# Local attention block: a second buffer for the cosine products of k and for its weights, and the probabilities multiplied on GpSimd

## The reference, cut to what matters

```python
def attn_layer(x, Wqkv, qs, ksc, Wo):
    q, k, v = jnp.split(x @ Wqkv, 3, -1)          # then 16 heads of 64
    q = l2norm(q) * qs
    k = l2norm(k) * ksc
    q = q * cos * scale + rotate_half(q) * sin * scale
    k = k * cos * inv + rotate_half(k) * sin * inv
    out = local_attention(q, k, v)                # softmax over 64 keys per query
    return out @ Wo

for i in range(DEPTH):                            # 6
    x = attn_layer(shift_tokens(x), Wqkv[i], ...) + x
    x = ffn_layer(shift_tokens(x), ...) + x
```

## Time and profile before

| | |
|---|---|
| median of 3 runs | 4544.87 us (4536.48 to 4553.36) |
| the profiled execution, its time | 4562.02 us |
| the profiled execution, its span | 4560.2 us |
| mean granted TensorE clock | 0.959 of full speed |
| first local block, `by_cosine` of k first and last | 591 us to 2214 us |
| second local block, the same | 2849 us to 4471 us |

### The profile page before, as it was taken

One profiled execution on the slowest core, in us unless ns is written; L12 is line 12 of the kernel. 1 busy time (PEld: TensorE's weight loads), 2 busy tenths in 40 slices (PEclk: granted clock), 3 DMA queues, 4 the chain that ended last, 5 costly groups with the idle time before them and its releaser, 6 DMA issues. The chain is left out here.

```text
span 4560.2 us, 151802 instructions
## 1 busy us (share of the span) xinstructions
PE 4106.5 (90%) x66856; PEld 2986.7 (65%) x66856; DVE 3629.6 (80%) x4427; ACT 2586.8 (57%) x3022; POOL 2608.7 (57%) x3233
## 2 busy tenths in 40 slices
PE   8999968999999999999878887798999999999997
PEld 5665557777777777777633333677777777777775
DVE  5536568888888898898668884888888888888885
ACT  3414335666666656656427773465656656566664
POOL 2103167677767766767424441776767767677673
PEclk8989989999999999999969997999999999999999
DMA  4304232323223232232100001223232232323221
GB/s 143 118 10 151 86 94 65 90 70 90 65 70 93 67 87 68 74 87 69 38 10 1 1 1 39 72 58 98 66 89 72 69 86 67 92 68 91 66 67 37
DMA packets 164545, 316.97 MB, mean 70 GB/s; under 512 B 38760, under 2 KB 42480, under 8 KB 156848
## 3 DMA queue, kind: packets, MB, share of 16 engines
q1 hardware_dynamic: 153520, 241.18, 19.8%
q0 software_dynamic: 10368, 66.06, 4.5%
HBM read 92.03 MB, written 20.05 MB: 25 GB/s over the span
## 5 line engine op out<-in xcount | busy, mean ns | idle before, releaser
L695 PE MATMUL psum<-loc_w_hl,loc_z_lo 128*128 128x512 f32 x1152 | 513.9, 446 | 33.5 <-DMA loc_w_hl<-parted 25.3
L1077 POOL TENSOR_TENSOR loc_rc_k<-loc_rc_k,loc_rs_k 128x1024 f32<-128x1024 f32 x192 | 456.5, 2378 | 85.2 <-DVE loc_rs_k L1187 84.8
L697 PE MATMUL psum<-loc_w_hl,loc_z_hi 128*128 128x512 f32 x1152 | 460.5, 400 | 5.9 <-issue 5.7
L1077 POOL TENSOR_TENSOR loc_rc_q<-loc_rc_q,loc_rs_q 128x1024 f32<-128x1024 f32 x192 | 464.4, 2419 | 0.0
L1173 DVE TENSOR_REDUCE loc_ssq<-loc_sq 128x16 f32<-128x1024 f32 x384 | 463.6, 1207 | 0.0
L696 PE MATMUL psum<-loc_w_hl,loc_z_hi 128*128 128x512 f32 x1152 | 460.4, 400 | 1.3 <-issue 1.3
L941 ACT ACTIVATE loc_sq<-psum 128x1024 f32<-128x1024 f32 x192 | 196.6, 1024 | 466.9 <-PE psum L697 461.9
L1168 DVE TENSOR_TENSOR loc_rc_k<-psum,loc_rot 128x1024 f32<-128x1024 f32 x192 | 234.6, 1222 | 257.2 <-POOL loc_qk_k L1083 227.9
L792 PE MATMUL psum<-loc_PT,loc_V 64*64 64x32 f32 x24576 | 407.1, 220 | 15.3 <-issue 15.0
L792 PEld LDWEIGHTS psum<-loc_PT,loc_V 64*64 64x64 f32 x24576 | 383.3, 135 | 41.6 <-issue 18.2
L812 PEld LDWEIGHTS psum<-loc_outT,loc_wo 128*128 128x128 f32 x3072 | 382.3, 196 | 25.5 <-issue 8.6
(11 more groups left out here) (198 smaller groups left out, 9914.2 us busy)
## 6 DMA issues: line engine op xcount, KB each, us to landing
loc_V<-loc_V SPq DMA_DIRECT2D x1152, 128.0 KB, 2.3
loc_V<-loc_V SPq DMA_DIRECT2D x672, 64.0 KB, 2.0
loc_w_hl<-parted POOLq DMA_DIRECT2D x36, 1024.0 KB, 7.3
parted<-moe_halves POOLq DMA_DIRECT2D x18, 1024.0 KB, 5.2
moe_spread<-moe_gates SPq DMA_DIRECT2D x64, 256.0 KB, 4.1
moe_raw<-in_wqkv POOLq DMA_DIRECT2D x18, 512.0 KB, 5.9
moe_w<-in_moe_w SPq DMA_DIRECT2D x32, 256.0 KB, 3.6
loc_wo<-in_wo SPq DMA_DIRECT2D x12, 512.0 KB, 3.7
```

The costliest lines, as they stand in the source:

```text
L695: pe.matmul(M.bank[bank + g], z_lo[:, r, tokens], w_hl[:, k, 0, cols], start=True, stop=False)
L697: mm = pe.matmul(M.bank[bank + g], z_hi[:, r, tokens], w_hl[:, k, 0, cols], start=False, stop=True)
L1077: pool.tensor_tensor(rc[:, :], rc[:, :], rs[:, :], ALU.add).then_inc(added, 1)
```

## The change

`rc_k` and the weights of k get a second buffer each; `by_cosine` of k waits for k_ready of the tile before the last; VectorE waits for root_ready ahead of `total_squares` of k and for k_added ahead of `by_sine` of k; the weights of k of the next layer are loaded in step 8, into slot 3 for odd layers; `normalise` goes from VectorE to GpSimd, between `scaled` of q for n-1 and `total_of` k for n.

```diff
@@ -551,7 +551,7 @@
         pe_passed, pool_passed, sp_passed = (sem(n) for n in ("pe_passed", "pool_passed", "sp_passed"))
 
         zs = M.zs
-        w_hl = sb("w_hl", [P, 3, 2, INNER], F32R)
+        w_hl = sb("w_hl", [P, 4, 2, INNER], F32R)
         z_bits = sb("z_bits", [P, T])
         z_hi, z_lo = (sb(n, [P, 2, T], F32R) for n in ("z_hi", "z_lo"))
         wo = sb("wo", [P, PAIRS, D])
@@ -561,7 +561,8 @@
         scales = sb("scales", [P, 4, DH])
         rot = sb("rot", [P, 4, TILES, DH])
         minus_half = sb("minus_half", [P, TILES])
-        sq, rc_q, rc_k, rs_q, rs_k = (sb(n, [P, INNER]) for n in ("sq", "rc_q", "rc_k", "rs_q", "rs_k"))
+        sq, rc_q, rs_q, rs_k = (sb(n, [P, INNER]) for n in ("sq", "rc_q", "rs_q", "rs_k"))
+        rc_k = sb("rc_k", [P, 2, INNER])
         ssq, rn, rt, ru = (sb(n, [P, 2 * HEADS]) for n in ("ssq", "rn", "rt", "ru"))
         qk_q, qk_k = (sb(n, [P, PAIRS, 2, DH]) for n in ("qk_q", "qk_k"))
         qT = sb("qT", [P, PAIRS, P])
@@ -714,7 +715,7 @@
                 else:
                     pe.wait_ge(k_rotated, upto(L, t - 1))
                     pe.wait_ge(kT_ready, upto(L, t - 2))
-                project(XB, t, 1, k_full)
+                project(XB, t, 1 if L % 2 == 0 else 3, k_full)
 
             def project_v(L, t, full):
                 if t == 0:
@@ -1035,7 +1036,8 @@
             pool.sem_inc(gate_full, CREDIT * FBLK)
             pool.sem_inc(lin_full, CREDIT * FBLK)
             def load_parts(L, k, loaded):
-                pool.dma_start(w_hl[:, k, :, :], M.parted[L, :, k, :, :]).then_inc(loaded, 16)
+                slot = 3 if k == 1 and L % 2 else k
+                pool.dma_start(w_hl[:, slot, :, :], M.parted[L, :, k, :, :]).then_inc(loaded, 16)
 
             load_parts(0, 1, wk_loaded)
             load_parts(0, 2, wv_loaded)
@@ -1074,13 +1076,13 @@
 
             def total_of(L, t, rotated, rc, rs, added):
                 pool.wait_ge(rotated, upto(L, t))
-                pool.tensor_tensor(rc[:, :], rc[:, :], rs[:, :], ALU.add).then_inc(added, 1)
+                pool.tensor_tensor(rc, rc, rs[:, :], ALU.add).then_inc(added, 1)
 
             def scaled(L, t, added, turned, rc, a, out, ready):
                 pool.wait_ge(root_ready, L * TS + (t + 1))
                 pool.wait_ge(added, L * TS + (t + 1))
                 pool.wait_ge(turned, upto(L, t - 1))
-                pool.tensor_tensor(pair_major(out[:, :, :, :]), by_pair(rc[:, :]), spread_heads(rn[:, a:a + HEADS], DH),
+                pool.tensor_tensor(pair_major(out[:, :, :, :]), by_pair(rc), spread_heads(rn[:, a:a + HEADS], DH),
                                    ALU.mult).then_inc(ready, 1)
 
             def rest_of_tokens(L, s):
@@ -1088,6 +1090,11 @@
                 if L * SEQS + s >= 2:
                     pool.wait_ge(q_full, upto(L, (s - 1) * TILES - 1))
                 pool.tensor_tensor(z_lo[:, s % 2, :], zs[:, s, 0:T], z_bits[:, :], ALU.subtract).then_inc(z_split, 1)
+
+            def normalise(L, t):
+                pool.wait_ge(recip_ready, upto(L, t))
+                both = pair_major(prob[:, :, :, :])
+                pool.tensor_tensor(both, both, spread_heads(recip[:, :], 2 * WINDOW), ALU.mult).then_inc(p_ready, 1)
 
             def deviation(L, t):
                 s = t // TILES
@@ -1110,18 +1117,20 @@
                     load_parts(L, 0, wq_loaded)
                 if live(n - 1):
                     root(L, n - 1)
-                if n == TS - 1 and L + 1 < DEPTH:
-                    pool.wait_ge(k_full, upto(L, n))
+                if n == TS // 2 and L + 1 < DEPTH:
+                    pool.wait_ge(k_full, upto(L, -1))
                     load_parts(L + 1, 1, wk_loaded)
                 if live(n - 1):
-                    scaled(L, n - 1, k_added, tk_full, rc_k, HEADS, qk_k, k_ready)
-                    total_of(L, n - 1, q_rotated, rc_q, rs_q, q_added)
-                    scaled(L, n - 1, q_added, tq_full, rc_q, 0, qk_q, q_ready)
+                    scaled(L, n - 1, k_added, tk_full, rc_k[:, (n - 1) % 2, :], HEADS, qk_k, k_ready)
+                    total_of(L, n - 1, q_rotated, rc_q[:, :], rs_q, q_added)
+                    scaled(L, n - 1, q_added, tq_full, rc_q[:, :], 0, qk_q, q_ready)
                 if n == TS - 1 and L + 1 < DEPTH:
                     pool.wait_ge(v_full, upto(L, n))
                     load_parts(L + 1, 2, wv_loaded)
+                if live(n - 2):
+                    normalise(L, n - 2)
                 if live(n):
-                    total_of(L, n, k_rotated, rc_k, rs_k, k_added)
+                    total_of(L, n, k_rotated, rc_k[:, n % 2, :], rs_k, k_added)
                 if n % TILES == 2 and L < DEPTH:
                     after, s = divmod(n // TILES + 1, SEQS)
                     if L + after < DEPTH:
@@ -1162,10 +1171,10 @@
                 dve.tensor_scalar(z_bits[:, :].bitcast(I32), zs[:, s, 0:T].bitcast(I32), LOW_BITS, None,
                                   ALU.bitwise_and).then_inc(z_cut, 1)
 
-            def by_cosine(L, t, c, squared, bank, rc, ready):
+            def by_cosine(L, t, c, squared, bank, rc, ready, before):
                 dve.wait_ge(squared, upto(L, t))
-                dve.wait_ge(ready, upto(L, t - 1))
-                dve.tensor_tensor(heads(rc[:, :]), heads(bank),
+                dve.wait_ge(ready, upto(L, t - before))
+                dve.tensor_tensor(heads(rc), heads(bank),
                                   rot[:, c, t % TILES, :].rearrange("p (o d) -> p o d", o=1).broadcast_to([P, HEADS, DH]),
                                   ALU.mult)
 
@@ -1208,11 +1217,6 @@
             def invert(L, t):
                 dve.wait_ge(p_summed, upto(L, t))
                 dve.reciprocal(recip[:, :], total[:, :]).then_inc(recip_ready, 1)
-
-            def normalise(L, t):
-                dve.wait_ge(recip_ready, upto(L, t))
-                both = pair_major(prob[:, :, :, :])
-                dve.tensor_tensor(both, both, spread_heads(recip[:, :], 2 * WINDOW), ALU.mult).then_inc(p_ready, 1)
 
             def add_attention(L, t):
                 s, i = t // TILES % SEQS, t % TILES
@@ -1258,8 +1262,12 @@
                 if live(n):
                     if n == 0:
                         factors(L)
-                    by_cosine(L, n, 2, k_squared, X_, rc_k, k_ready)
+                    by_cosine(L, n, 2, k_squared, X_, rc_k[:, n % 2, :], k_ready, 2)
+                    if n or L:
+                        dve.wait_ge(root_ready, L * TS + n)
                     total_squares(L, n, HEADS, k_totalled)
+                    if n or L:
+                        dve.wait_ge(k_added, L * TS + n)
                     by_sine(L, n, 3, X_, rs_k, k_rotated)
                 if live(n - 9) and lasts(n - 9):
                     hidden(L, n - 9, 2)
@@ -1270,13 +1278,12 @@
                 if live(n - 2):
                     sum_probs(L, n - 2)
                     invert(L, n - 2)
-                    normalise(L, n - 2)
                 if live(n - 5) and lasts(n - 5):
                     take_variance(L, n - 5)
                 if live(n - 8) and lasts(n - 8):
                     hidden(L, n - 8, 1)
                 if live(n):
-                    by_cosine(L, n, 0, q_squared, W_, rc_q, q_ready)
+                    by_cosine(L, n, 0, q_squared, W_, rc_q[:, :], q_ready, 1)
                     total_squares(L, n, 0, q_totalled)
                 if live(n - 7) and lasts(n - 7):
                     hidden(L, n - 7, 0)
```

## The result

The changed kernel takes 4390.78 us (median of 4 runs, 4381.30 to 4397.17) against 4549.11 us for the kernel before (4 runs too, with one more than in the table above). The ratio of the runs is 0.9652, 95% interval 0.9620 to 0.9684: 158 us, 3.5% faster. The forecast was 93 us and its range ended at 4418: right in direction, too small in size.

A forecast was written before the change was run, and what follows sets the result against it. TensorE was taken as the floor, only its waits to be won: 102 us of waits plus 15 in the ramps minus 24 of give-back, 93 us off 4545, gives 4452 us; range 4418 to 4520.

The forecast's parts named there:

- What bounds: Local block's steps: TensorE is the floor, 15.79 of 16.55 us a step; only what it waits for can be won.
- Two buffers: `rc_k`: the cosine product of k no longer waits for `scaled`, so VectorE's chain through the attention's sum is 1.2 us earlier.
- The multiply: `normalise` on POOL: 1.90 us, with 4.17 as the other end; L819's and L869's waits on TensorE go.
- give-back: Gaps in TensorE's stream at L766 take back 24 us in 84 steps, with 0 and 116 us as ends.
- L825's 44.7 the layer starts stay: TensorE's variance wait: of 44.7 us, ten layer starts at 1.61 stay and 28.6 go.
- The ramps: About 12 steps where TensorE isn't the floor: the guess loop falls away, POOL's 15.2 replaces 16.5, worth 15 us.
- The fourth slot: `w_hl`: loading w_k in step 8 instead of 15 costs nothing, as layer starts aren't waiting for it.
- The marks: Signs in the new profile: right if L819, L859, L869 waits go; wrong if L702, L766 or root_ready waits show.
- A: POOL's long steps aren't given back by its short ones: 31 to 66 us lost, 4483 to 4518; chance 0.18.
- B: Gaps in TensorE's stream fill what the waits leave: 116 us for 24, 4544, no change; chance 0.09.
- C: `normalise` on POOL costs per element what `rest_of_tokens` does; POOL becomes the bound at 17.5 us a step: 4705; chance 0.06.
- D: Sum of squares waits for the root instead, `normalise` is as late as before: no effect, 4545; chance 0.04.

## Why the prediction was right in direction and too small

- **What bounds.** Right. TensorE is the floor and VectorE's lateness costs what is above it; undoing part of that lateness moves the time, as the two buffers alone show, and the multiply alone once it is queued last.
- **Two buffers.** Right in mechanism. I had not asked what each part is worth without the other. The loop over the multiply, which with this order on POOL only the two buffers open, was not in the prediction. Nor was it said that POOL's later sum would hold up `floored`.
- **The multiply.** Taken at 1.90, measured at 1.91. The 2.44 estimated from the Trainium skill's factor of about two (GPSIMD Engine Reference, Engine selection) would have been 28% too dear. The factor fits POOL's sum of two full operands, 2.37 us, 1.94 times VectorE's 1.22. The rows of 1.9 us have one operand broadcast from 16 values; that this is the reason was not tested.
- **The sum.** The direction was right and the size too small by some 40%. In the two windows the time fell by 163.4 us: idle 125.1, busy 38.3. With its give-back at 0 the forecast's own sum would have ended at 117 us, so even that bound was short. Against the forecast's 93:
  - "L825's 44.7 the layer starts stay" failed: 40.5 went, not 28.6. That is 12 us. By the timeline only 11.2 of the 44.7 lay in first steps (seven waits), and of these 4.2 are left. First steps fell from 21.95 to 20.84 us on average.
  - The ramps and the turns: L702's three waits for VectorE and POOL, 28.1 and, by the same view, 25.1 and 6.8, fell to 12.7, 9.5 and 15.6, 22 us for the 15.
  - The give-back was 10 us at L766, not 24.
  - The step that failed most is the prediction's first, on what bounds the kernel: TensorE's busy time was taken as its work, so that each removed wait was priced at its idle row alone. The floor of 15.79 us a step held some 0.2 us that was no work, 38.3 us in all (at most 5.5 of it the clock). That is some 0.3 us for each of the 130 waits that went at L819, L825, L859 and L869, and the run with `hidden` late brings 15.1 us back for 44 waits, 0.34 each. The term was put at nothing, without a reason.
  - Together 12 + 7 + 14 + 38 = 71, which with 93 makes 164, for a measured 163.4. The rows are totals over the run and not over the windows, so that it comes out so closely is in part chance.
- **The fourth slot.** Nothing, as said.
- **The marks.** Nearly all those given for "right" are met: L819 gone and L859 and L869 but for 2 us, L825 but for 4.2 us gone, kinds 0 and 3, where they have no gap, at 16.3 and 15.5, even below the 16.9 and 15.9 named, for the reason above. The first steps did not stay as before. Of the marks for "wrong", none: L702 waits 12.7 us, L766's gaps are 64, and VectorE's wait for root_ready is 4.3 us on the page.
- **The rivals.** A had POOL's long steps cost 31 to 66 us; a further microsecond a step on POOL cost 34 in all, most of it in first steps, so that at 1.9 the ordinary steps paid next to nothing. B: gaps did rise, by 10 us. C fell with the multiply's duration and D with the waits; C's price rested on a row that was itself held up (see the last section). The range was too narrow below: it let every removed wait count for no more than its row.

## What to carry to other kernels

When an instruction goes to another engine, ask whose queue it then delays: with one buffer, the same multiply on the same engine was worth 0 or 143 us, by which side of one sum it stood on. Two remedies for one loop don't add up; price each one with and without the other. Where matmuls follow each other closely, compare steps with and without the wait, start to start, and don't take the busy time for the work. Compare the durations of the other engines' instructions before and after too: one that is held up gets longer and shows no wait.

## What was not expected of the hardware

- A wait of TensorE costs more than its idle row: 15.1 us of busy time for 44 waits that show 73.1 us, and 0.89 us for a row of 0.72.
- Gaps in TensorE's stream and its waits stand in for one another: 1 us more on POOL made 55 us of waits and took 52 us of gaps away. Why is not shown.
- The gap in `values` came at the end of 5 us with 263 GB/s of transfers, and TensorE's clock was at its lower level for 7 us behind it. With 1 MB of the loads moved away the first steps got 1.6 us shorter, and 1.3 us more with the other order on POOL; that the loads alone cause the gap was not shown.
- `rest_of_tokens` on POOL ran 2.09 us beside VectorE's multiply and 1.19 without it; VectorE's multiply had run 1.66 us beside POOL's work, at best 1.22. Each of the two held the other up. The Trainium skill (SBUF — State Buffer, Who interferes with whom) has this as an exclusive lock; the trace agrees. In the prediction I took the 2.09 us for a rate per element and built the upper end, 4.17, and rival C on it. It was a wait.
- The hold-up is not limited to instructions with two inputs: `floored`, a `tensor_scalar` of 128x32 on one tile, took 0.18 us in the kernel before and up to 2.05 after, and 135 of its 136 long ones end with an instruction of POOL.
